# Per-image statistics moved into PSUM, gelu moved behind a unit's second bias, and the measuring steps spread out, in a fused group norm and directional convolution

## The chip, the cores and the metric

The kernel runs on one core of one Trainium2 chip. The metric is the device time of one execution, in microseconds (us). Engines are named as in the profile: PE is TensorE's matmul side, PEld its weight loads, DVE is VectorE, ACT is ScalarE, POOL is GpSimd, SP is SyncE (DMA queues have a q behind the name).

## The reference

x has the shape (16, 256, 56, 56), float32: 16 images of 256 channels.

```python
xn  = group_norm(x)                          # 32 groups of 8 channels, eps 1e-5, no affine part
h   = depthwise_conv3x3(xn, dw_weight)       # zero padding 1
h   = gelu(h)                                # the exact one
maps = einsum('bchw,oc->bohw', h, pw_weight) + pw_bias     # 256 -> 8 * 256 channels
out = x
for i, (dx, dy) in enumerate(OFFSETS8):      # the 8 neighbours
    out += maps[:, i] * (roll(xn, (dy, dx)) - xn)
```

The group norm's scale is taken out of the differences: they are made of x, and the maps are multiplied by 1/std, together with the bias.

## The kernel before

The 256 channels are two halves of 128 partitions. An image has 7 tiles of 8 rows (448 pixels); a **body** is two images, 14 tiles, and there are 8 bodies. Each engine runs its own program, written out in order by hand, and engines meet only in semaphores.

Per tile, TensorE makes eight **units** (`make_maps`, L880). A unit is a pair of directions in one half of the channels, two **sides** of 448 columns, one PSUM bank each. A side is six matmuls of 128x128 by 448: weights and h are split into a high and a low part, and three of the four products are taken for each half of the input channels. Eight units are 16 groups of six, 96 matmuls. The units use three pairs of banks in turn (`GROUPS`, L64; banks 0 to 5), with one exception: the last four units of a body take the pairs 0, 1, 0, 2. Before a unit TensorE waits until VectorE is done with the last user of its pair (L887). Banks 6 and 7 hold the convolution's sums.

ScalarE adds the bias and scales each side in place (`add_bias`, L578, the activation at L586). VectorE multiplies a unit with the difference fields, per tile in this order (L846 to L874): `first_product` of units 0 and 1, written to the sums (L690, acc); `second_product` of unit 2, written back in place (L690, psum), and `second_add`, which adds it to the sums and frees the banks (L712); `kept_product` of units 3 to 7, written to SBUF (L690, products), which GpSimd adds to the sums (`add_pair`, L365). Between these VectorE puts the eight taps of the convolution for the tile three ahead (`tap`, L770; for an image's last tile, made in its fourth, each tap is two instructions of half the size, L761).

The convolution's chain crosses the engines: ScalarE normalises x into xn (L542); the centre tap starts the sums (`start_conv`, L561; L557 in two halves); VectorE's eight taps follow; then ScalarE's gelu empties banks 6 and 7 (L571), its copy to the high part is L576, and GpSimd makes the low part (L334). gelu has to wait for the last tap, the next centre tap for gelu, and the next first tap for the centre tap. In ScalarE's body (L608 to L621) these stand behind the bias of a numbered unit:

```python
GELU_AT, START_AT, HHI_AT, NORM_AT = 0, 1, 2, 7
```

The statistics of the next image are made beside this. ScalarE measures it in twelve steps (`measure_step`, L477: sums, minus the mean, squares, variance, for each half), four in each of tiles 0, 1 and 2. VectorE then turns the moments of 128 channels into group statistics in ten small instructions on 32 or fewer columns (`group_stats`, L627 to L672: two transposes in, sums over 8, differences, their squares and sums, transposes back). They are drawn one at a time by `stats_next()`, from behind unit 6's product in tile 2 on into tile 3. All their operands are in SBUF. GpSimd makes 1/std, shift and bias of the result (`norm_scales`, L319).

GpSimd further makes the difference fields (L346, L350) and issues the DMAs that add the sums to out (L372). SyncE loads an image two ahead in the sixth tile (L286 to L289).

Of the kernel before, what the change touches and what calls it, by code (L numbers as in the profile page):

```python
# [5 lines left out]
def preact_directional_conv(nc, x, pw_t, pw_b, dw, out):  # L6
# [4 lines left out]
    P = 128  # L11
    B, C, H, W = x.shape
# [3 lines left out]
    TILES = H // ROWS  # L16
    PX = ROWS * W
# [61 lines left out]
    with ctx:  # L79
        def sb(name, shape, dt=F32):  # L80
            return ctx.enter_context(nc.sbuf_tensor(name, shape, dt))
# [46 lines left out]
        sums = sb("sums", [P, 4])  # L128
        mean_t = sb("mean_t", [P, 32])
        dev_t = sb("dev_t", [P, 32])  # L130
        devs_t = sb("devs_t", [P, 32])
        mean_b = sb("mean_b", [P, 32])
        devs_b = sb("devs_b", [P, 32])
        var_eps = sb("var_eps", [P, HALVES])
# [3 lines left out]

        psum = ctx.enter_context(nc.psum_tensor("psum", [P, 8, BANK], F32))

        def rows_of(par, g, c):
# [88 lines left out]
        MEASURES = HALVES * HALF_STEPS  # L230
        STAT = 10
        SCALES = 3
# [15 lines left out]

        GELU_AT, START_AT, HHI_AT, NORM_AT = 0, 1, 2, 7
        WRAP_AT = (4, 3)  # L250
        MEASURE_AT = ((0, 3), (0, 4), (0, 5), (0, 6), (1, 3), (1, 4), (1, 5), (1, 6), (2, 2), (2, 3), (2, 4), (2, 5))
        STATS_TILE, SCALES_TILE = 2, 3
# [192 lines left out]
        def _(act):  # L445
# [132 lines left out]
            def add_bias(n0, nl, u):  # L578

                ip, q = (nl // TILES) % 2, nl * UNITS + u  # L580
                for side in range(2):
# [5 lines left out]
                                         scale=rstd[ip][:, g:g + 1]).then_inc(biased_s, 1)  # L587

            measure_first()
            wrap(0, 0)  # L590
# [13 lines left out]
            def body(n0, b0, last):  # L604
                for nl in range(STEPS):
                    t, par = nl % TILES, nl // TILES
                    more = lambda k: not (last and nl + k >= STEPS)
                    for u in range(UNITS):  # L608
                        add_bias(n0, nl, u)
                        if (t, u) in MEASURE_AT and not (last and par):  # L610
                            measure_step(b0 + par + 1, 1 - par, MEASURE_AT.index((t, u)))
                        if u == GELU_AT and more(2):
# [13 lines left out]
        def _(dve):  # L626
            def group_stats(b):  # L627
# [4 lines left out]
                def then(ins):  # L632
                    ins.then_inc(stat, 1)
                    done[0] += 1
# [14 lines left out]
                wait()  # L649
                then(nc.vector.tensor_scalar(by8(mean_t[:]), wide(sums[:]), 1.0 / GROUP, None, ALU.mult))  # L650
                yield
                wait()
                then(nc.vector.tensor_tensor(dev_t[:], mom_t[:], mean_t[:], ALU.subtract))  # L653
                yield
                wait()
                then(nc.vector.tensor_tensor(dev_t[:], dev_t[:], dev_t[:], ALU.mult))
                yield
                wait()
                then(nc.vector.reduce_sum(sums[:], by8(dev_t[:]), axis=AX.X))
                yield  # L660
                wait()
                then(nc.vector.tensor_scalar(by8(devs_t[:]), wide(sums[:]), 1.0 / GROUP, None, ALU.mult))  # L662
                yield
                wait()
                then(nc.vector.transpose(mean_b[:], mean_t[:]))
                yield
                then(nc.vector.transpose(devs_b[:], devs_t[:]))
                yield
# [164 lines left out]
            def body(n0, b0, last):  # L833
                nonlocal stats
                for nl in range(STEPS):
# [7 lines left out]
                    if last and nl == STEPS - 1:  # L843
                        last_tile(n0, nl)
                        return
                    first_product(n0, nl, 0)  # L846
                    stats_next()
                    first_product(n0, nl, 1)
                    stats_next()
                    tap_next()  # L850
                    second_product(n0, nl)
                    tap_next()
                    second_add(n0, nl)
# [18 lines left out]
                    tap_next()  # L872
                    stats_next()
                    stats_next()  # L874

# [60 lines left out]
```

## Time and profile before

| | |
|---|---|
| three runs | 2354.85, 2356.59, 2357.29 us |
| median | 2356.59 us |
| profiled execution, its own time | 2353.0 us |
| its span in the profile | 2351.2 us |
| mean granted TensorE clock | 0.989 of full |
| PE busy | 2227.3 us, 95% |
| DVE busy | 2159.4 us, 92% |
| POOL busy | 1979.9 us, 84% |
| ACT busy | 1826.8 us, 78% |
| DMA engines | 86 GB/s on average |

The profile is of one execution; the span is what lies between its first and last instruction. Matmuls overlap, so PE's rows last longer (370 ns) than the distance from one to the next (203 ns); a group of six takes 1.22 us. A row of VectorE or ScalarE also overlaps the next by some 0.1 us.

### The profile page before, as it was taken

What the parts mean: (1) busy time and instruction counts of PE and PEld (TensorE: products, weight loads), DVE (VectorE), ACT (ScalarE), POOL (GpSimd) and SP (SyncE); (2) the same over time, 40 slices, a digit from 0 to 9 for tenths busy, and PEclk for the clock granted to TensorE, in tenths of its full rate; (3) what the DMA queues carried; (4) which work ended last, traced back from release to release, by engine and by line L of the source; (5) the groups of instructions that cost most, each with busy time, mean ns of one, the idle gap of its engine ahead of it and who ended that gap; (6) DMA issues with size and microseconds to landing.
All of it is one profiled execution on the core that took longest, in us unless ns stands there. A gap on an engine that the chain in (4) does not pass through costs nothing.

```text
span 2351.2 us, 28668 instructions
## 1 busy us (share of the span) xinstructions
PE 2227.3 (95%) x10752; PEld 2031.0 (86%) x10752; DVE 2159.4 (92%) x2218; ACT 1826.8 (78%) x2762; POOL 1979.9 (84%) x857
## 2 busy tenths in 40 slices
PE   2999999999999999999999999999999999999998
PEld 1889898898988989899898888989889898898997
DVE  7999999999999999999999999999999999999995
ACT  5968778787887968779687796877878788797775
POOL 5879898897978989799897997989879898898985
PEclk9999999999999999999999999999999999999999
DMA  6234263442725426153361643526344272543413
GB/s 187 45 71 110 48 124 73 87 95 47 159 38 102 94 48 149 32 103 93 62 135 32 118 94 66 115 45 110 89 85 96 48 151 46 95 93 51 98 32 71
DMA packets 47083, 202.13 MB, mean 86 GB/s; under 512 B 3040, under 2 KB 7136, under 8 KB 45664
## 3 DMA queue, kind: packets, MB, share of 16 engines
q0 software_dynamic: 30192, 94.97, 24.8%
q1 hardware_dynamic: 16752, 105.34, 17.3%
q8 instruction: 84, 1.38, 0.2%
q14 instruction: 55, 0.45, 0.1%
HBM read 104.88 MB, written 146.80 MB: 107 GB/s over the span
## 4 chain that ended last, share of the span: by engine, by line
PE 57%; DVE 27%; ACT 11%; issue 5%; DMA 0%; SPq 0%; DVEq 0%
PE psum L898 57%; DVE psum L770 6%; DVE products L690 6%; DVE psum L761 5%; ACT psum L586 5%; ACT squares_out L469 2%; DVE dev_t L653 2%; DVE acc L690 2%; DVE psum L690 2%; DVE acc L712 1%; ACT hid L571 1%; ACT squares_out L459 1%; DVE devs_t L662 1%; DVE var_eps L670 1%; ACT psum L561 1%
## 5 line engine op out<-in xcount | busy, mean ns | idle before, releaser
L586 ACT ACTIVATE psum<-psum,bias,rstd 128x448 f32<-128x448 f32 x1792 | 1214.0, 700 | 399.2 <-PE psum L898 396.9
L365 POOL TENSOR_TENSOR acc<-acc,products 128x896 f32<-128x896 f32 x333 | 1166.9, 3504 | 321.5 <-DVE products L690 315.0
L898 PE MATMUL psum<-hhi,w_hi 128*128 128x448 f32 x3584 | 1326.0, 370 | 117.1 <-DVE acc L690 46.1
L898 PE MATMUL psum<-hhi,w_lo 128*128 128x448 f32 x3584 | 1321.9, 369 | 0.0
L898 PE MATMUL psum<-hlo,w_hi 128*128 128x448 f32 x3584 | 1028.8, 368 | 0.3 <-POOL hlo L334 0.3
L770 DVE SCALAR_TENSOR_TENSOR psum<-xn,dw_f,psum 128x896 f32<-128x896 f32 x768 | 881.4, 1148 | 3.5
L898 PEld LDWEIGHTS psum<-hhi,w_hi 128*128 128x128 f32 x3584 | 677.9, 189 | 193.3 <-DVE acc L690 51.7
L898 PEld LDWEIGHTS psum<-hhi,w_lo 128*128 128x128 f32 x3584 | 679.7, 190 | 59.4
L898 PEld LDWEIGHTS psum<-hlo,w_hi 128*128 128x128 f32 x3584 | 677.7, 189 | 60.6 <-POOL hlo L334 0.9
L690 DVE TENSOR_TENSOR products<-psum,fields 128x896 f32<-128x896 f32 x555 | 602.1, 1085 | 49.6 <-ACT psum L586 48.2
L690 DVE TENSOR_TENSOR acc<-psum,fields 128x896 f32<-128x896 f32 x224 | 243.4, 1087 | 119.1 <-ACT psum L586 119.1
L334 POOL TENSOR_TENSOR hlo<-hid,hhi 128x896 fp32r<-128x896 f32 x112 | 264.9, 2365 | 12.9 <-ACT hhi L576 12.9
L350 POOL TENSOR_TENSOR fields<-xpad 128x896 f32<-128x896 f32 (+1 forms) x112 | 240.1, 2144 | 0.0
L346 POOL TENSOR_TENSOR fields<-xpad 128x912 f32<-128x912 f32 (+1 forms) x112 | 209.8, 1874 | 0.0
L571 ACT ACTIVATE hid<-psum 128x896 f32<-128x896 f32 x112 | 103.2, 922 | 108.8 <-DVE psum L770 71.9
L761 DVE SCALAR_TENSOR_TENSOR psum<-xn,dw_f,psum 128x448 f32<-128x448 f32 x256 | 160.4, 676 | 0.0
L372 POOL DMA_DIRECT2D out<-acc x111 | 132.8, 1197 | 7.9 <-DMA out<-acc 7.3
L690 DVE TENSOR_TENSOR psum<-psum,fields 128x896 f32<-128x896 f32 x117 | 128.4, 1098 | 5.9 <-ACT psum L586 4.7
L712 DVE TENSOR_TENSOR acc<-psum,acc 128x896 f32<-128x896 f32 x111 | 120.3, 1084 | 0.2
L542 ACT ACTIVATE xn<-xpad,shift,rstd 128x1008 f32<-128x1008 f32 (+1 forms) x96 | 116.8, 1217 | 0.0
L576 ACT CAST hhi<-hid 128x896 fp32r<-128x896 f32 x112 | 106.7, 953 | 0.0
L561 ACT ACTIVATE psum<-xn,dw_f 128x896 f32<-128x896 f32 x96 | 98.2, 1023 | 0.1
(66 smaller groups left out, 558.1 us busy)
## 6 DMA issues: line engine op xcount, KB each, us to landing
out<-acc POOLq DMA_DIRECT2D x96, 896.0 KB, 7.7
out<-x SPq DMA_DIRECT2D x16, 3136.0 KB, 12.5
xpad<-x SPq DMA_DIRECT2D x30, 1568.0 KB, 14.9
out<-acc POOLq DMA_DIRECT2D x15, 448.0 KB, 5.6
acc<-x SPq DMA_DIRECT2D x4, 784.0 KB, 7.0
xpad<-pw_t SPq DMA_DIRECT2D x1, 2048.0 KB, 12.0
out<-products SPq DMA_DIRECT2D x2, 224.0 KB, 1.9
dw_f<-dw SPq DMA_DIRECT2D x1, 9.0 KB, 8.0
```

What stands on the lines that cost most here:

```text
L334: nc.gpsimd.tensor_tensor(hlo[:, slot], hid[:], hhi[:, slot].bitcast(F32), ALU.subtract).then_inc(hlo_s, 1)
L346: nc.gpsimd.tensor_tensor(gx[:, :, f + 2 * lo:f + TR, :], v[:, :, r + 2 * lo:r + TR, 1:WP], v[:, :, r + 2 * lo:r + TR, 0:WP - 1], ALU.subt ...
L350: nc.gpsimd.tensor_tensor(gy[:, :, f + lo:f + ROWS + 1, :], v[:, :, r + lo + 1:r + TR, 1:W + 1], v[:, :, r + lo:r + ROWS + 1, 1:W + 1], AL ...
L365: nc.gpsimd.tensor_tensor(a, a, p, ALU.add).then_inc(added_s, 1)
L372: pool.dma_start(out_dst[b, :, :, t * PX:(t + width) * PX], acc[buf][:, :, sign].rearrange("p g t x -> p g (t x)"), accum_op=ALU.add).then ...
L571: nc.scalar.activation(hid[:], conv_of(n0, c), ACT.Gelu).then_inc(gelu_s, 1)
L586: nc.scalar.activation(m, m, ACT.Identity, bias=bias[ip][:, g, d:d + 1], scale=rstd[ip][:, g:g + 1]).then_inc(biased_s, 1)
L690: return nc.vector.tensor_tensor(to.rearrange("p s (r c) -> p s r c", c=W), maps(q).rearrange("p s (r c) -> p s r c", c=W), field, ALU.mult)
L712: nc.vector.tensor_tensor(a, maps(nl * UNITS + u), a, ALU.add).then_inc(prod_s, 1)
L761: nc.vector.scalar_tensor_tensor(d, xn[c % 2][:, g * TR + ky:g * TR + ky + ROWS, kx:kx + W], dw_f[:, g, TAPS_DVE[j]:TAPS_DVE[j] + 1], d, A ...
L770: nc.vector.scalar_tensor_tensor(d, xn[c % 2][:, ky:ky + 2 * ROWS, kx:kx + W].rearrange("p (a r) c -> p a r c", a=2), dw_f[:, g, TAPS_DVE[ ...
L898: last = nc.tensor.matmul(maps(q)[:, side, :], w[:, kk, col:col + P], h_part(h, t, nl, kk), start=s == 0, stop=s == len(steps) - 1)
```

## The change

It has three parts.

1. **Statistics in PSUM.** `mean_t`, `dev_t`, `devs_t` and `devs_b` leave SBUF for the 64 columns of banks 6 and 7 that the convolution leaves free (448 to 511). The squaring of the differences now takes `dev_t` from PSUM and a second copy, `dev_s`, from SBUF; making it is one more instruction (`STAT` is 11). The small instructions are drawn at other places of the tile: none stands between the last tap and the next first tap, in which time ScalarE uses banks 6 and 7.
2. **gelu** moves from behind unit 0's bias to behind unit 1's, in front of the centre tap (`GELU_AT` 0 to 1).
3. **Measuring** spreads over four tiles: three steps each in the last tile of the image before and in tiles 0, 1 and 2. For the second image the old places stay (`MEASURE_SECOND`).

```diff
-        mean_t = sb("mean_t", [P, 32])
-        dev_t = sb("dev_t", [P, 32])
-        devs_t = sb("devs_t", [P, 32])
+        dev_s = sb("dev_s", [P, 32])
         mean_b = sb("mean_b", [P, 32])
-        devs_b = sb("devs_b", [P, 32])
...
+        mean_t, dev_t, devs_t, devs_b = (psum[:, CONV_BANK + i // 2, PX + 32 * (i % 2):PX + 32 * (i % 2 + 1)]
+                                         for i in range(4))
...
-        STAT = 10
+        STAT = 11
...
-        GELU_AT, START_AT, HHI_AT, NORM_AT = 0, 1, 2, 7
+        GELU_AT, START_AT, HHI_AT, NORM_AT = 1, 1, 2, 7
...
-        MEASURE_AT = ((0, 3), (0, 4), (0, 5), (0, 6), (1, 3), (1, 4), (1, 5), (1, 6), (2, 2), (2, 3), (2, 4), (2, 5))
+        MEASURE_AT = ((-1, 4), (-1, 6), (-1, 6), (0, 3), (0, 5), (0, 5), (1, 3), (1, 5), (1, 5), (2, 3), (2, 5), (2, 5))
+
+        MEASURE_SECOND = ((0, 3), (0, 4), (0, 5), (0, 6), (1, 3), (1, 4), (1, 5), (1, 6), (2, 2), (2, 3), (2, 4), (2, 5))
...
+            def measure_at(n, u):
...
+                b, t = divmod(n, TILES)
+                if t == TILES - 1:
+                    b, t = b + 1, -1
+                if b + 1 < B:
+                    places = MEASURE_AT if b else MEASURE_SECOND
+                    for i in range(MEASURES):
+                        if places[i] == (t, u):
+                            measure_step(b + 1, (b + 1) % 2, i)
...
                         add_bias(n0, nl, u)
-                        if (t, u) in MEASURE_AT and not (last and par):
-                            measure_step(b0 + par + 1, 1 - par, MEASURE_AT.index((t, u)))
+                        measure_at(n0 + nl, u)
...
-                then(nc.vector.tensor_tensor(dev_t[:], mom_t[:], mean_t[:], ALU.subtract))
+                then(nc.vector.tensor_tensor(dev_t, mom_t[:], mean_t, ALU.subtract))
+                then(nc.vector.tensor_tensor(dev_s[:], mom_t[:], mean_t, ALU.subtract))
                 yield
                 wait()
-                then(nc.vector.tensor_tensor(dev_t[:], dev_t[:], dev_t[:], ALU.mult))
+                then(nc.vector.tensor_tensor(dev_t, dev_t, dev_s[:], ALU.mult))
...
-                then(nc.vector.transpose(mean_b[:], mean_t[:]))
-                yield
-                then(nc.vector.transpose(devs_b[:], devs_t[:]))
+                then(nc.vector.transpose(mean_b[:], mean_t))
+                then(nc.vector.transpose(devs_b, devs_t))
...
                     first_product(n0, nl, 0)
+                    first_product(n0, nl, 1)
+                    tap_next()
                     stats_next()
-                    first_product(n0, nl, 1)
+                    second_product(n0, nl)
                     stats_next()
                     tap_next()
-                    second_product(n0, nl)
-                    tap_next()
+                    stats_next()
                     second_add(n0, nl)
...
                     kept_product(n0, nl, 7)
                     tap_next()
-                    stats_next()
-                    stats_next()
```

VectorE from unit 6's product in an image's third tile to unit 2's product in the fourth, in the kernel before:

```order
L690 TENSOR_TENSOR products<-psum,fields 128x896
L770 SCALAR_TENSOR_TENSOR psum<-xn,dw_f,psum 128x2x448
L653 TENSOR_TENSOR dev_t<-mom_t,mean_t 128x32
L656 TENSOR_TENSOR dev_t<-dev_t 128x32
L690 TENSOR_TENSOR acc<-psum,fields 128x2x448
L659 TENSOR_REDUCE sums<-dev_t 128x4
L690 TENSOR_TENSOR acc<-psum,fields 128x2x448
L662 TENSOR_SCALAR devs_t<-sums 128x32
L761 SCALAR_TENSOR_TENSOR psum<-xn,dw_f,psum 128x448 x2
L690 TENSOR_TENSOR psum<-psum,fields 128x2x448
```

and the same place with the change, up to the second addition (here L705 is the product, L785 and L776 are the taps, L727 the second addition; small instructions with psum are those on mean_t, dev_t and devs_t):

```order
L705 TENSOR_TENSOR products<-psum,fields 128x896
L785 SCALAR_TENSOR_TENSOR psum<-xn,dw_f,psum 128x2x448
L705 TENSOR_TENSOR acc<-psum,fields 128x2x448 x2
L776 SCALAR_TENSOR_TENSOR psum<-xn,dw_f,psum 128x448 x2
L668 TENSOR_TENSOR psum<-mom_t,psum 128x32
L669 TENSOR_TENSOR dev_s<-mom_t,psum 128x32
L705 TENSOR_TENSOR psum<-psum,fields 128x2x448
L672 TENSOR_TENSOR psum<-psum,dev_s 128x32
L776 SCALAR_TENSOR_TENSOR psum<-xn,dw_f,psum 128x448 x2
L675 TENSOR_REDUCE sums<-psum 128x4
L727 TENSOR_TENSOR acc<-psum,acc 128x2x448
```

The first products stand together in front of the first tap, and the small instructions that stood around them come behind it. The big instructions keep their order.

ScalarE at the start of a tile, in the kernel before (L586 is the bias, two to a unit):

```order
L586 ACTIVATE psum<-psum,bias,rstd 128x448 x2
L571 ACTIVATE hid<-psum 128x896
L586 ACTIVATE psum<-psum,bias,rstd 128x448 x2
L561 ACTIVATE psum<-xn,dw_f 128x2x448
L586 ACTIVATE psum<-psum,bias,rstd 128x448 x2
L576 CAST hhi<-hid 128x896
```

and with the change (L590 bias, L575 gelu, L565 centre tap):

```order
L590 ACTIVATE psum<-psum,bias,rstd 128x448 x4
L575 ACTIVATE hid<-psum 128x896
L565 ACTIVATE psum<-xn,dw_f 128x2x448
L590 ACTIVATE psum<-psum,bias,rstd 128x448 x2
L580 CAST hhi<-hid 128x896
```

gelu has gone from between the biases of units 0 and 1 to behind both, and now stands directly in front of the centre tap that waits for it.

## Rows read from the trace of the kernel before

**Rows 1.** The list of waits: engine and line, releaser, us in total, times, longest.

```profile
PE psum L898 <- DVE acc L690: 46.1, 15, 3.4
PE psum L898 <- DVE acc L712: 24.3, 30, 2.1
```

**Rows 2.** Timeline of PE: start us, us, engine, line, operation, count [idle before, releaser].

```profile
113.68 0.57 PE L898 MATMUL psum<-hlo,w_hi 128*128 128x448 f32 x2
...
1123.98 0.47 PE L898 MATMUL psum<-hhi,w_hi 128*128 128x448 f32 x1 [3.37 <-DVE acc L690]
...
2128.64 0.57 PE L898 MATMUL psum<-hlo,w_hi 128*128 128x448 f32 x2
```

**Rows 3.** Two stretches: length, busy us per engine, granted clock, DMA share, GB/s.

```profile
1125.00:1128.40 3.40, 3.40 (x11) 3.05 (x10) 3.40 (x5) 0.88 (x2) 1.89 (x1) 0.53 0.00 0
721.62:832.02 110.40, 110.40 (x542) 101.23 (x540) 101.53 (x99) 92.27 (x139) 99.11 (x41) 1.00 0.51 104
```

**Rows 4.** Timeline of PE in an undisturbed tile: its first and sixth unit.

```profile
1035.05 0.36 PE L898 MATMUL psum<-hhi,w_hi 128*128 128x448 f32 x1
...
1047.25 0.36 PE L898 MATMUL psum<-hhi,w_hi 128*128 128x448 f32 x1
```

**Rows 5.** Timeline of DVE around the statistics of one image.

```profile
1113.18 0.20 DVE L644 STREAM_TRANSPOSE mom_t<-moments 128x32 f32<-128x32 f32 x1
1113.31 1.11 DVE L770 SCALAR_TENSOR_TENSOR psum<-xn,dw_f,psum 128x896 f32<-128x896 f32 x1
...
1115.52 0.18 DVE L650 TENSOR_SCALAR mean_t<-sums 128x32 f32<-128x32 f32 x1
...
1117.66 3.22 DVE L653 TENSOR_TENSOR dev_t<-mom_t,mean_t 128x32 f32<-128x32 f32 x1
...
1122.85 1.08 DVE L690 TENSOR_TENSOR acc<-psum,fields 128x896 f32<-128x896 f32 x1
...
1129.04 1.26 DVE L761 SCALAR_TENSOR_TENSOR psum<-xn,dw_f,psum 128x448 f32<-128x448 f32 x2
```

**Rows 6.** Timeline of POOL at the same time.

```profile
1116.78 4.05 POOL L365 TENSOR_TENSOR acc<-acc,products 128x1792 f32<-128x1792 f32 x1 [0.28 <-DVE products L690]
```

**Rows 7.** Groups by line and form: busy us, mean ns of one, idle before.

```profile
L653 DVE TENSOR_TENSOR dev_t<-mom_t,mean_t 128x32 f32<-128x32 f32 x16 | 48.5, 3033 | 0.0
L662 DVE TENSOR_SCALAR devs_t<-sums 128x32 f32<-128x32 f32 x16 | 28.4, 1775 | 0.0
L656 DVE TENSOR_TENSOR dev_t<-dev_t 128x32 f32<-128x32 f32 x16 | 27.3, 1707 | 0.5
...
L670 DVE SCALAR_TENSOR_TENSOR var_eps<-mean_b,devs_b 128x2 f32<-128x2 f32 x16 | 15.5, 971 | 0.0
...
L737 DVE TENSOR_TENSOR acc<-acc,xpad 128x896 f32<-128x896 f32 x1 | 1.1, 1082 | 0.0
```

**Rows 8.** Timeline of DVE in the undisturbed tile: units 1 and 2.

```profile
1041.21 1.09 DVE L690 TENSOR_TENSOR acc<-psum,fields 128x896 f32<-128x896 f32 x1 [1.20 <-ACT psum L586]
...
1043.38 1.10 DVE L690 TENSOR_TENSOR psum<-psum,fields 128x896 f32<-128x896 f32 x1
...
1045.44 1.08 DVE L712 TENSOR_TENSOR acc<-psum,acc 128x896 f32<-128x896 f32 x1
```

**Rows 9.** Timeline of ACT in the undisturbed tile, from the last bias of the tile before.

```profile
1035.26 0.70 ACT L586 ACTIVATE psum<-psum,bias,rstd 128x448 f32<-128x448 f32 x1 [0.52 <-PE psum L898]
...
1039.05 0.93 ACT L571 ACTIVATE hid<-psum 128x896 f32<-128x896 f32 x1 [0.66 <-DVE psum L770]
1039.87 1.31 ACT L586 ACTIVATE psum<-psum,bias,rstd 128x448 f32<-128x448 f32 x2
1041.09 1.02 ACT L561 ACTIVATE psum<-xn,dw_f 128x896 f32<-128x896 f32 x1
1042.02 1.32 ACT L586 ACTIVATE psum<-psum,bias,rstd 128x448 f32<-128x448 f32 x2
```

**Rows 10.** DMA issues of the page: KB each, us to landing.

```profile
xpad<-x SPq DMA_DIRECT2D x30, 1568.0 KB, 14.9
```

More of the change, by code:

```diff
@@ L649, in group_stats @@
                 wait()
-                then(nc.vector.tensor_scalar(by8(mean_t[:]), wide(sums[:]), 1.0 / GROUP, None, ALU.mult))
+                then(nc.vector.tensor_scalar(by8(mean_t), wide(sums[:]), 1.0 / GROUP, None, ALU.mult))
                 yield
                 wait()
-                then(nc.vector.tensor_tensor(dev_t[:], mom_t[:], mean_t[:], ALU.subtract))
+                then(nc.vector.tensor_tensor(dev_t, mom_t[:], mean_t, ALU.subtract))
+                then(nc.vector.tensor_tensor(dev_s[:], mom_t[:], mean_t, ALU.subtract))
                 yield
                 wait()
-                then(nc.vector.tensor_tensor(dev_t[:], dev_t[:], dev_t[:], ALU.mult))
+                then(nc.vector.tensor_tensor(dev_t, dev_t, dev_s[:], ALU.mult))
                 yield
                 wait()
-                then(nc.vector.reduce_sum(sums[:], by8(dev_t[:]), axis=AX.X))
+                then(nc.vector.reduce_sum(sums[:], by8(dev_t), axis=AX.X))
                 yield
                 wait()
-                then(nc.vector.tensor_scalar(by8(devs_t[:]), wide(sums[:]), 1.0 / GROUP, None, ALU.mult))
+                then(nc.vector.tensor_scalar(by8(devs_t), wide(sums[:]), 1.0 / GROUP, None, ALU.mult))
                 yield
                 wait()
-                then(nc.vector.transpose(mean_b[:], mean_t[:]))
-                yield
-                then(nc.vector.transpose(devs_b[:], devs_t[:]))
+                then(nc.vector.transpose(mean_b[:], mean_t))
+                then(nc.vector.transpose(devs_b, devs_t))
                 yield
```

## The prediction

> **What bounds the kernel now.** By the page's first part TensorE is busy for 95% of the span, so the time is TensorE's work plus its pauses. The list of waits says who pauses it inside the loop: 46.1 us in 15 waits for VectorE's first product (L690), and 24.3 us in 30 waits for the second addition at L712 [rows 1]. Fifteen is the number of images measured inside the loop, so the pauses belong to the statistics, not to the tiles.
>
> The timeline of TensorE places them: in one image a unit's first matmul comes at 1123.98 after 3.37 us idle [rows 2], and the L712 waits, 0.81 on average, follow as one in that tile and one in the next. Behind the long pause the granted clock of 1125.00 to 1128.40 is 0.53, against 1.00 in an undisturbed stretch [rows 3]: nearly all of it at the lower level, 1.2 GHz, after the engine had stood idle. From 113.68 to 2128.64, the last matmuls before the first and the fifteenth long pause [rows 2], are 14 periods, 143.93 us each. What would seven undisturbed tiles take? A tile is 16 groups of six matmuls. Ninety groups took 110.40 us from 721.62 [rows 3], 1.227 each; ten took 12.20 from 1035.05 to 1047.25 [rows 4], 1.220 each. So 112 groups take 136.6 to 137.4 us, and I take 137.1, between the two paces. **Lost are 6.8 us per image, 102 us over 15 images**: the three pauses, the refilling behind each, and the half clock.
>
> Why the long pause? VectorE's timeline beside GpSimd's gives it. L653 subtracts 32 columns in 3.22 us and ends at 1120.88 [rows 5]; GpSimd's addition, begun at 1116.78 for 4.05, ends at 1120.83 [rows 6]. L650, of the same form as the slow L662, took 0.18 at 1115.52 [rows 5], before that addition began. Over the run L653 means 3033 ns, L662 1775, L656 1707, L670 971 [rows 7]: together 7.5 us an image, for work that takes 0.2 each when unhindered. All four have only SBUF operands. Instructions with one tensor in PSUM run beside GpSimd's at their usual length all the time: the taps, L690 in place 1.10, L712 1.08 [rows 8]. Behind the four stands the product at 1122.85 [rows 5], 1.08 long, whose end lets TensorE go at 1123.98.
>
> **The change, part by part.** *Statistics.* Each instruction that was blocked now has a tensor in PSUM. I take 0.12 us of VectorE each, as L644 at 1113.18 let the tap start at 1113.31 [rows 5]. No row shows these very forms; the bounds are 0.1 and, should they block, what they cost now (1.0 to 3.2 us). I take the low end, since every form with a PSUM tensor in the trace runs at it. That is 1.3 us an image for eleven, beside VectorE's idle time of 1.20 in front of each second product [rows 8] and more behind it; if that cover went, TensorE would wait for L712 (below).
>
> A rule of the Trainium skill speaks against this: "VectorE: DVE Perf Modes", section on the TRN2 errata, gives a VectorE operation from PSUM a fixed 120 cycles where one from SBUF has 58; by it, eight small instructions per image would cost an estimated 65 ns more each, 8 us over the run if nothing hid them. The trace does not agree: an addition of 896 columns with SBUF operands alone takes 1082 ns [rows 7], the PSUM product of the same width 1.10 us [rows 8], a difference of 0.02.
>
> *Measuring.* The twelve ScalarE steps keep their durations and go to earlier tiles, at most three to one. ScalarE waits for TensorE in most units, 0.52 us before 1035.26 [rows 9], so they cost nothing; uncovered, one would delay a product by up to 1.6 us, which still has about 2 us until its banks are wanted. Where the steps begin in the seventh tile two images ahead, the load of x was issued in the sixth, behind the differences made early in it; it lands in 14.9 us [rows 10], and the step comes over 20 us after the issue. Nothing is lost.
>
> *Gelu behind the second bias.* This touches every tile, so I follow one. Its first matmul is at 1035.05, a side follows every 1.22 us, and the sixth unit, at 1047.25 [rows 4], reuses the banks that L712 frees. Now: gelu waits for the last tap until 1039.05, second bias 1039.87, centre tap 1041.09, third bias 1042.02 [rows 9], second unit's product 1041.21, third unit's 1043.38, L712 at 1045.44 for 1.08 [rows 8], ended 1046.52: 0.7 us in hand. After: the second unit is complete at 1035.05 + 4 x 1.22 = 1039.93. ScalarE starts its last bias 0.20 later, as 1035.26 stands to 1035.05: 1040.13. Gelu follows by 0.61 (the spacing of a bias and the centre tap, 1040.48 to 1041.09), 1040.74, for 0.93; the centre tap waits for it, 1041.70; the third biases come 0.93 behind, 1042.63, for 1.32, until 1043.95. Product 1043.99, L712 2.06 later as in rows 8: 1046.05, ended 1047.13. TensorE resumes 0.05 behind such an end (1123.98 against 1123.93), and the first matmul after a wait takes 0.47 for 0.36, 0.11 more [rows 2, 4]: 1047.29 against 1047.25. **So the new order loses about 0.04 us a tile, 4 us in 108 tiles**, and uses up the margin. Bounds: 0, and 0.3 if gelu's 0.93 came onto the old chain in full (0.93 less 0.7, and the restart). I take what I added up, since each link is a row.
>
> *The fourth tile of an image* has sixteen half taps. Until L712 it has one pair of halves, 1.26 against 1.11 to 1.15 for a whole [rows 5], so 0.12 more; two small instructions in front of L712, 0.24; and a centre tap in two halves on ScalarE, 0.17 more. 0.53 us, times 15 is 8 us (bounds 0 and 1.0 each). The halves and small ones behind L712, 1.2 us, fit into VectorE's idle time.
>
> *The last tile of every second image*: there the bank table puts the seventh unit onto the fifth's banks, two units back instead of three. The fifth product starts 3.06 behind L712 (one spacing of 1.00 and one of 2.06), at 1049.11 in the tile above, ends at 1050.19 and lets TensorE go by 1050.35; wanted is 1035.05 + 12 x 1.22 = 1049.69. 0.65 x 7 = 4.6 us, where the old chain just did it (bounds 0 and 1.0 each).
>
> Sum: -102 + 4 + 8 + 4.6 + 0.3 (one instruction more before the loop) = -85. The span goes from 2351.2 to 2266, the profiled execution's own time from 2353.0 to 2268; the median shown is 3.6 above that, so **2271 us**. Late next is L712 in every tile, by next to nothing, and then TensorE's own pace.
>
> **Rivals.**
> 1. *The gelu chain is some tenths longer than added up* (a link that no row shows, ScalarE held by its new neighbours). Every 0.1 a tile is 11 us; at 0.3 the time is 2304. For: no margin is left. Against: the links are measured. Chance 0.15.
> 2. *The chain is much longer, and the kernel slower.* Place: the third unit's bias, queued on ScalarE behind gelu and centre tap. From 0.8 us of lateness a tile more than added up (0.8 x 108 = 86) it takes all that the statistics give; at 1.0 the time is 2379. For: gelu and centre tap together are 1.95 us, so the price is there. Against: old and new chain hold the same instructions, and end 0.6 apart. Chance 0.04.
> 3. *Small instructions are still blocked.* If all are, the long pause and its half clock stay, 16 us of third pauses go at best and the chain's 17 come: 2357, chance 0.04. If only the multiplication by 1/8 of sums (old L662), of which no PSUM form is in the trace: it now stands ahead of a product with 1.9 us of margin, and the time is below 2285, chance 0.08.
> 4. *No pause anywhere, the chain and the tiles with halves included*: 2271 - 17 = 2254, and at the faster pace throughout 6 less, 2248. Chance 0.12.
>
> **The numbers.** The forecast itself, about 2258 to 2285, has 0.57. The range takes in rival 1 up to its 0.3, the small block of rival 3 and the upper half of rival 4: 2252 to 2302. Faster, same and slower part at 0.2%, 5 us, about what a measurement of this kernel can tell. Faster 0.92 (the forecast, rivals 1 and 4, the small block of 3), same 0.03 (most of the large block), slower 0.05 (rival 2 and the rest).
>
> **What would show it.** The statistics' lines at 0.2 us; no TensorE wait for a first product inside the loop; a granted clock of 1.00 through the fourth tile; 138 us per image; VectorE's wait of 1.20 down to about 0.5, and a new one of about 0.8 in front of the first tap; gelu without a wait for taps; the end of L712 within 0.1 us of the sixth unit's matmul; short waits for it in fourth tiles, and one for the fifth product per two images. Wrong it would be if small instructions still last over a microsecond, if TensorE waits for L712 by over 0.2 us in every tile, or if ScalarE waits for x in the seventh tile.

## The result and the profile after

| | before | after |
|---|---|---|
| runs | 2354.85 to 2357.29 us | 2269.90 to 2271.90 us (4 runs) |
| median | 2356.18 us | **2271.43 us** |
| profiled execution, its own time / its span | 2353.0 / 2351.2 us | 2271.6 / 2269.8 us |
| mean granted clock | 0.989 | 0.999 |
| PE busy | 95% | 97% |
| DVE / ACT / POOL busy | 92% / 78% / 84% | 91% / 81% / 87% |

The ratio is 0.9639 (95% interval 0.9623 to 0.9656): 3.6% faster, 0.4 us from the forecast. That the hit is so close is partly chance. The two spans differ by 81.4 us where the sum said 85, so the span came at 2269.8 where 2266 was forecast. What made up for it is the 3.6 us that the forecast added for the distance between the profiled execution of before and its median: the profiled execution of after (2271.6) lies on its median. Three executions of the kernel of experiment 5 (2344.87, 2528.48 and 2529.34 us) were disturbed as a whole and are left out of its figures.

The list of waits of after (engine and line, releaser, us in total, times, longest), which answers to [rows 1]. The old L690 is now L705, L712 is L727, L770 is L785, L586 is L590, L571 is L575.

```profile
DVE psum L785 <- ACT psum L565: 79.5, 93, 1.1
...
PEld psum L913 <- DVE acc L727: 28.3, 109, 0.7
...
ACT hid L575 <- DVE psum L785: 12.0, 2, 6.5
...
PE psum L913 <- DVE acc L727: 4.7, 15, 0.3
PE psum L913 <- DVE products L705: 2.4, 7, 0.4
```

Of 70.4 us of TensorE's waits in [rows 1] 4.7 are left, and new are seven of 0.35. No wait for a first product (L705, acc) is there. TensorE's weight load waits for L727 109 times, 0.26 on average: in every tile the second addition now ends at the last moment. gelu (L575) waits for taps twice in the whole run. The first tap of a tile (L785) waits 0.85 on average, 93 times, for the centre tap.

The timeline of TensorE answers to [rows 2, 4]. Columns as there.

```profile
118.86 0.57 PE L913 MATMUL psum<-hlo,w_hi 128*128 128x448 f32 x2
...
1055.94 0.36 PE L913 MATMUL psum<-hhi,w_hi 128*128 128x448 f32 x1
...
1068.13 0.47 PE L913 MATMUL psum<-hhi,w_hi 128*128 128x448 f32 x1
...
1087.46 0.57 PE L913 MATMUL psum<-hlo,w_hi 128*128 128x448 f32 x2
1088.32 0.47 PE L913 MATMUL psum<-hhi,w_hi 128*128 128x448 f32 x1 [0.29 <-DVE acc L727]
...
1149.51 0.57 PE L913 MATMUL psum<-hlo,w_hi 128*128 128x448 f32 x2
1150.43 0.47 PE L913 MATMUL psum<-hhi,w_hi 128*128 128x448 f32 x1 [0.35 <-DVE products L705]
...
2056.53 0.57 PE L913 MATMUL psum<-hlo,w_hi 128*128 128x448 f32 x2
```

From 118.86 to 2056.53 are again 14 images: 138.41 us each, against 143.93. Times 15 that is 82.8 us, so the loop holds the whole difference of the spans, 81.4. The short pause of 0.29 us at 1088.32 is all that is left in this tile, where before paused for 3.37. The clock does not fall behind it: the window around it (columns of [rows 3]) has a granted clock of 1.00, where before had 0.53, and so has the whole tile, 1076 to 1096.

```profile
1087.00:1092.00 5.00, 4.71 (x24) 3.99 (x23) 5.00 (x12) 2.63 (x4) 5.00 (x4) 1.00 0.01 3
```

The groups of VectorE by form answer to [rows 7]:

```profile
L672 DVE TENSOR_TENSOR psum<-psum,dev_s 128x32 f32<-128x32 f32 x16 | 3.0, 190 | 0.0
L668 DVE TENSOR_TENSOR psum<-mom_t,psum 128x32 f32<-128x32 f32 x16 | 3.0, 190 | 0.0
...
L678 DVE TENSOR_SCALAR psum<-sums 128x32 f32<-128x32 f32 x16 | 3.0, 187 | 0.0
...
L685 DVE SCALAR_TENSOR_TENSOR var_eps<-mean_b,psum 128x2 f32<-128x2 f32 x16 | 2.5, 153 | 0.0
```

The four that took 3033, 1707, 1775 and 971 ns take 190, 190, 187 and 153. VectorE's and GpSimd's timelines of one image's fourth tile show them beside GpSimd's work, which goes on without a break [rows 5, 6].

```profile
1084.20 0.19 DVE L668 TENSOR_TENSOR psum<-mom_t,psum 128x32 f32<-128x32 f32 x1
1084.30 0.18 DVE L669 TENSOR_TENSOR dev_s<-mom_t,psum 128x32 f32<-128x32 f32 x1
...
1085.81 0.19 DVE L672 TENSOR_TENSOR psum<-psum,dev_s 128x32 f32<-128x32 f32 x1
...
1087.19 1.08 DVE L727 TENSOR_TENSOR acc<-psum,acc 128x896 f32<-128x896 f32 x1
```
```profile
1083.50 2.08 POOL L350 TENSOR_TENSOR fields<-xpad 128x1140 f32<-128x1140 f32 x1
1085.55 2.00 POOL L354 TENSOR_TENSOR fields<-xpad 128x1008 f32<-128x1008 f32 x1
1087.52 2.10 POOL L338 TENSOR_TENSOR hlo<-hid,hhi 128x896 fp32r<-128x896 f32 x1
```

An ordinary tile, on ScalarE and on VectorE; these answer to [rows 8, 9], and the tile's first matmul is the one at 1055.94.

```profile
1061.02 0.70 ACT L590 ACTIVATE psum<-psum,bias,rstd 128x448 f32<-128x448 f32 x1 [0.52 <-PE psum L913]
1061.65 0.91 ACT L575 ACTIVATE hid<-psum 128x896 f32<-128x896 f32 x1
1062.65 1.01 ACT L565 ACTIVATE psum<-xn,dw_f 128x896 f32<-128x896 f32 x1
1063.60 1.30 ACT L590 ACTIVATE psum<-psum,bias,rstd 128x448 f32<-128x448 f32 x2
```
```profile
1061.75 1.09 DVE L705 TENSOR_TENSOR acc<-psum,fields 128x896 f32<-128x896 f32 x1 [0.24 <-ACT psum L590]
1063.70 1.16 DVE L785 SCALAR_TENSOR_TENSOR psum<-xn,dw_f,psum 128x896 f32<-128x896 f32 x1 [0.85 <-ACT psum L565]
1064.93 1.10 DVE L705 TENSOR_TENSOR psum<-psum,fields 128x896 f32<-128x896 f32 x1
1065.94 1.15 DVE L785 SCALAR_TENSOR_TENSOR psum<-xn,dw_f,psum 128x896 f32<-128x896 f32 x1
1066.99 1.08 DVE L727 TENSOR_TENSOR acc<-psum,acc 128x896 f32<-128x896 f32 x1
```

L727 ends at 1068.07, and the sixth unit starts at 1068.13. Counted from the tile's first matmul, the end is at 12.13, 0.07 before TensorE wants the banks (10 x 1.22 = 12.20). One line stands between the product at 1064.93 and the addition: the second tap, 1.05 us. The experiments come back to it.

### The profile page after: what moved, and what is told of

Read it like the earlier page. It is cut to its first block, busy times and chain, and to the rows that moved or that the text cites. A ratio compares the mean times of both kernels' runs of the same rounds, so it can differ in the third digit from the quotient of the medians.

```text
span 2269.8 us, 28684 instructions
## 1 busy us (share of the span) xinstructions
PE 2209.1 (97%) x10752; PEld 2008.5 (88%) x10752; DVE 2056.1 (91%) x2234; ACT 1844.6 (81%) x2762; POOL 1981.4 (87%) x857
## 4 chain that ended last, share of the span: by engine, by line
PE 88%; DVE 5%; ACT 4%; issue 2%; DMA 0%; POOL 0%; SPq 0%; ACTq 0%; DVEq 0%
PE psum L913 88%; ACT psum L590 1%; DVE psum L705 1%; ACT hid L575 1%; DVE psum L785 1%; ACT psum L561 1%; DVE acc L727 1%; DVE products L705 1%; DVE psum L776 1%; DMA acc<-x 0%; ACT psum L565 0%; DVE acc L757 0%; POOL hlo L338 0%; DVE fields L808 0%; DVE part_sums L795 0%
## 5 line engine op out<-in xcount | busy, mean ns | idle before, releaser
L590 ACT ACTIVATE psum<-psum,bias,rstd 128x448 f32<-128x448 f32 x1792 | 1205.9, 694 | 384.6 <-PE psum L913 381.9
L785 DVE SCALAR_TENSOR_TENSOR psum<-xn,dw_f,psum 128x896 f32<-128x896 f32 x768 | 883.1, 1150 | 83.0 <-ACT psum L565 79.5
L913 PEld LDWEIGHTS psum<-hhi,w_hi 128*128 128x128 f32 x3584 | 672.6, 188 | 137.1 <-issue 45.5
L913 PEld LDWEIGHTS psum<-hhi,w_lo 128*128 128x128 f32 x3584 | 672.8, 188 | 57.6
L705 DVE TENSOR_TENSOR products<-psum,fields 128x896 f32<-128x896 f32 x555 | 603.3, 1087 | 38.8 <-ACT psum L590 38.8
L705 DVE TENSOR_TENSOR acc<-psum,fields 128x896 f32<-128x896 f32 x224 | 242.6, 1090 | 53.2 <-ACT psum L590 51.8
L776 DVE SCALAR_TENSOR_TENSOR psum<-xn,dw_f,psum 128x448 f32<-128x448 f32 x256 | 161.6, 686 | 7.7 <-ACT psum L561 7.7
L705 DVE TENSOR_TENSOR psum<-psum,fields 128x896 f32<-128x896 f32 x117 | 128.6, 1100 | 17.9 <-ACT psum L590 10.8
L727 DVE TENSOR_TENSOR acc<-psum,acc 128x896 f32<-128x896 f32 x111 | 120.4, 1085 | 0.2
L575 ACT ACTIVATE hid<-psum 128x896 f32<-128x896 f32 x112 | 102.2, 913 | 12.0 <-DVE psum L785 12.0
L565 ACT ACTIVATE psum<-xn,dw_f 128x896 f32<-128x896 f32 x96 | 97.4, 1015 | 9.0 <-ACT hid L575 0.4
## 6 DMA issues: line engine op xcount, KB each, us to landing
xpad<-x SPq DMA_DIRECT2D x30, 1568.0 KB, 15.1
```

The costliest lines, as they stand in the source:

```text
L575: nc.scalar.activation(hid[:], conv_of(n0, c), ACT.Gelu).then_inc(gelu_s, 1)
L590: nc.scalar.activation(m, m, ACT.Identity, bias=bias[ip][:, g, d:d + 1], scale=rstd[ip][:, g:g + 1]).then_inc(biased_s, 1)
L705: return nc.vector.tensor_tensor(to.rearrange("p s (r c) -> p s r c", c=W), maps(q).rearrange("p s (r c) -> p s r c", c=W), field, ALU.mult)
L727: nc.vector.tensor_tensor(a, maps(nl * UNITS + u), a, ALU.add).then_inc(prod_s, 1)
L776: nc.vector.scalar_tensor_tensor(d, xn[c % 2][:, g * TR + ky:g * TR + ky + ROWS, kx:kx + W], dw_f[:, g, TAPS_DVE[j]:TAPS_DVE[j] + 1], d, A ...
L785: nc.vector.scalar_tensor_tensor(d, xn[c % 2][:, ky:ky + 2 * ROWS, kx:kx + W].rearrange("p (a r) c -> p a r c", a=2), dw_f[:, g, TAPS_DVE[ ...
```

## Experiments

Eleven kernels were run, one of them twice. The theory behind the prediction: the gain is the small instructions no longer blocked, the gelu move costs a little in every tile, and the measuring costs and gives nothing.

**1. Each part by itself.** First the measuring back at its old places, all else as after:

```diff
-                    places = MEASURE_AT if b else MEASURE_SECOND
+                    places = MEASURE_SECOND
```

> The changed kernel with the twelve measuring steps at the places of before for every image. My theory: they lie in ScalarE's waits either way: 2271.4 within 3 us. Rival, four steps in one tile delay biases and with them products: 5 us or more above.

Measured: 2271.34 us (2270.88 to 2271.97), ratio 0.9641 [0.9627, 0.9655], as after. The spreading gives nothing here, where gelu stands behind the second bias.

Then the four tiles back in SBUF, with the order of the instructions, gelu and the measuring as after:

```diff
-        mean_t, dev_t, devs_t, devs_b = (psum[:, CONV_BANK + i // 2, PX + 32 * (i % 2):PX + 32 * (i % 2 + 1)]
-                                         for i in range(4))
+        mean_t, dev_t, devs_t, devs_b = (sb(f"small{i}", [P, 32])[:] for i in range(4))
```

> The changed kernel with mean_t, dev_t, devs_t and devs_b in SBUF again, all else as changed. My theory: five or six small instructions wait for GpSimd's running one again, 1 to 3 us each; TensorE pauses for over 3 us per image and its clock falls behind that: 2350 to 2390. Rival, the new places of the small instructions in the tile brought the gain and PSUM did nothing: 2271 to 2285.

Measured: 2346.21 us (2342.71 to 2347.29), ratio 0.9954 [0.9939, 0.9969]. Its groups of VectorE by form:

```profile
L668 DVE TENSOR_TENSOR dev_s<-mom_t,small 128x32 f32<-128x32 f32 x16 | 29.3, 1831 | 0.0
L667 DVE TENSOR_TENSOR small<-mom_t,small 128x32 f32<-128x32 f32 x16 | 18.8, 1175 | 0.0
```

So the placement alone is worth 74.8 us (2346.21 - 2271.43) of the 84.8, and without it the other parts together bring 10. The new places in the tile are not what unblocked the statistics; with SBUF operands they are blocked there too, only the pause now comes at the second addition: 15 TensorE waits for it, 55.1 us in all. The time is 4 us under the range that was expected.

**2. Which forms are blocked?** Only `devs_t`, the result of the second multiplication by 1/8, goes back to SBUF. That instruction has one input tensor, not two:

```diff
+        devs_t = sb("devs_t", [P, 32])[:]
```

> The changed kernel with devs_t alone in SBUF again: L678, one input and one output in SBUF, no second tensor. My theory: it is blocked as L662 was, until the GpSimd instruction that runs at that time ends, 1 to 2 us on average, and as a product with 1.9 us of margin stands behind it, the time is 2271 to 2285. Rival, only instructions with two SBUF tensors as inputs are blocked: L678 at 0.19 us and 2271.4 within 2.

Measured: 2276.09 us (2275.29 to 2277.23), ratio 0.9661 [0.9647, 0.9676]. VectorE's group and its timeline, and GpSimd's:

```profile
L679 DVE TENSOR_SCALAR devs_t<-sums 128x32 f32<-128x32 f32 x16 | 18.3, 1141 | 0.0
```
```profile
1089.88 1.54 DVE L679 TENSOR_SCALAR devs_t<-sums 128x32 f32<-128x32 f32 x1
```
```profile
1089.28 2.10 POOL L339 TENSOR_TENSOR hlo<-hid,hhi 128x896 fp32r<-128x896 f32 x1
```

It ends at 1091.42, GpSimd's subtraction at 1091.38: the whole of the wait is that subtraction, and in all 15 images L679 ends 0.04 behind it. This form is blocked as well, and one such instruction costs 4.7 us over the run (2276.09 - 2271.43). In the kernel before, the sum over 8 (L647) and the transpose in front of it (L644, 0.20 us at 1113.18 [rows 5]) have only SBUF operands too, and run in the middle of a GpSimd addition without waiting for it:

```profile
1111.29 4.08 POOL L365 TENSOR_TENSOR acc<-acc,products 128x1792 f32<-128x1792 f32 x1 [1.52 <-DVE products L690]
```
```profile
1114.33 0.17 DVE L647 TENSOR_REDUCE sums<-mom_t 128x4 f32<-128x32 f32 x1
```

The Trainium skill has this in "SBUF — State Buffer", section "Who interferes with whom": an exclusive lock on a port pair shared with GpSimd, taken by a tensor_tensor with both inputs in SBUF (beside a GpSimd instruction that reads SBUF) and by a tensor_scalar in a two-port mode, never by tensor_reduce. By that rule the four tiles went to the right place, and these runs agree, 1141 ns for 32 columns among them. No transpose of these small tiles took over 0.22 us in any of the traces.

**3. What does the gelu move do, in the old kernel?** Before, with gelu behind the second bias and nothing else:

```diff
-        GELU_AT, START_AT, HHI_AT, NORM_AT = 0, 1, 2, 7
+        GELU_AT, START_AT, HHI_AT, NORM_AT = 1, 1, 2, 7
```

> The kernel before with gelu alone moved behind unit 1's bias. My theory: long pause, half clock and the pause at 0.8 us stay; the pause of the fifth tile (1.1 x 15 = 16 us) goes, 0.04 x 108 and 0.6 x 7 come: about 2348, between 2340 and 2360. Rival, the gelu move carries a good part of the 85 us: under 2320.

Measured: 2356.07 us (2354.77 to 2358.66, ten runs), ratio 1.0 [0.9991, 1.0009]. The expected gain of some 8 us did not come. Its waits, and the window behind the long pause of one image:

```profile
PE psum L898 <- DVE acc L690: 51.7, 15, 3.7
...
PE psum L898 <- DVE acc L712: 7.0, 10, 2.2
```
```profile
1128.00:1131.40 3.40, 3.40 (x11) 2.99 (x10) 3.40 (x5) 0.70 (x1) 2.01 (x1) 0.50 0.00 0
```

The waits for L712 fall from 24.3 us to 7.0: the pauses in the tile behind are gone, as expected. The long one grew, 46.1 to 51.7 in total, and the mean granted clock is lower, 0.985 for 0.989. Counted on TensorE from one tile's first matmul to the next's, on average over 14 images, the fifth tile of an image takes 19.67 us where before took 20.70, but the fourth 25.88 for 25.31, the last 19.95 for 19.59, and the other four about 0.07 more each: 1.0 us saved and 1.2 paid. The step that the expectation lacked is the longer fourth tile. A wait that goes can be paid back by the one beside it.

**4. The price of the gelu move without statistics.** Two kernels leave the statistics out from the second image on (VectorE only signals that they are done): before, and after.

```diff
+            def no_stats(b):
+
+                dve.wait_ge(measure, b * MEASURES + MEASURES)
+                dve.sem_inc(stat, STAT)
+                yield
...
-                        stats = iter(group_stats(b0 + par + 1))
+                        stats = iter(no_stats(b0 + par + 1))
```

> The kernel before without the ten small instructions for all images but the first (their semaphore is raised in one step; the later images are normalised with the first one's statistics); measuring stays. My theory: long pause, half clock and the pause in fourth tiles come from the small instructions and go, of the fifth tile's pause half stays: 2356 - 102 + 8 = 2262, between 2256 and 2268, with a granted clock of 1.00. Rival, the half clock comes once per image without the pause: 20 us more, about 2282. Second rival, the half taps cause the two pauses at L712 by themselves: 2275 or more.

> The changed kernel without the small instructions for all images but the first (as e5_before_no_stats). My theory: of the pause in fourth tiles (0.56 each) the 0.24 of the two small instructions in front of L727 goes, the rest is the gelu chain's: 2271.4 - 15 x 0.24 = 2267.8, between 2265 and 2270; against 2255.6 with gelu first this is the gelu move's own price, 12 us. Rival, the gelu chain costs nothing and the statistics are all that is left: 2256 to 2260.

Measured: before without statistics 2255.59 us (2255.20 to 2255.90), ratio 0.9574 [0.9558, 0.959]; after without them 2268.95 (2267.99 to 2269.45), 0.9633 [0.9619, 0.9647]. The first is just under the range expected. The statistics of before therefore cost 101 us (2356.18 - 2255.59), where the prediction had 102. Those of after cost 2.5. And the two kernels without statistics differ by **13.4 us**. They differ in the order of gelu and in the places of measuring, and measuring cost nothing in experiment 1, so the order of gelu is the likely price; the run that would part the two for certain (no statistics, gelu behind the second bias, measuring at the old places) was not made. Tile by tile (as in 3) the price lies in the fourth tile, 19.97 for 19.63 us, in the last, 19.95 for 19.61, and 0.04 in each of the others. The forecast had priced just this: 4 + 8 + 4.6 us, less 3.6 for the two small instructions, is 13.

**5. So put gelu back, with the small tiles in PSUM?** After, with one number changed:

```diff
-        GELU_AT, START_AT, HHI_AT, NORM_AT = 1, 1, 2, 7
+        GELU_AT, START_AT, HHI_AT, NORM_AT = 0, 1, 2, 7
```

> The changed kernel with gelu back behind unit 0's bias; statistics in PSUM and the new places of measuring stay. My theory: the gelu move did not bring the gain, it only lengthened every tile's chain by 0.6 us. Undone, L727 ends about 0.5 us before the sixth unit wants its banks, the 0.04 us per tile, the pause of the last tile of every second image (7 of 0.6) and most of the pause in fourth tiles (15 of 0.56) go, together 15 us; but in the fifth tile of an image gelu then waits for the late half taps, and up to 0.6 x 15 = 9 us come back there. 2263 to 2268. Rival, the move was needed: the third pause of 1.1 us per image returns in full and nothing goes, 2280 or more.

Measured: 2270.66 to 2272.31 us, ratio 0.964 [0.9624, 0.9656], where a gain was expected. It was run again, to read where the time lies:

> The same kernel as e1_gelu_first, which took 2272.15 us where I expected 2263 to 2268 and whose profile shows a disturbed TensorE. Time: 2272 again. What its profile is to tell: where the 16 us over e5_before_no_stats (2255.59, also gelu first) lie. Account A: in the fifth tile of an image gelu waits for the last half tap, the second bias stands behind gelu, and TensorE pauses for L727 by about 1 us, once per image. Account B: in the fourth tile, by the small instructions in front of L727. Account C: a little in every tile.

Measured: 2270.45 and 2271.76 us, ratio 0.9643 [0.9623, 0.9662]; span 2270.0 us against 2269.8. The moved gelu brings nothing in this kernel either, nor does it cost. The trace says why: two pauses stand in place of the small ones. The waits, and TensorE in the fourth tile and in the fifth:

```profile
ACT hid L575 <- DVE psum L785: 89.0, 82, 6.5
...
PE psum L913 <- DVE acc L727: 8.3, 21, 0.6
```
```profile
1088.69 0.47 PE L913 MATMUL psum<-hhi,w_hi 128*128 128x448 f32 x1 [0.49 <-DVE acc L727]
...
1108.02 0.57 PE L913 MATMUL psum<-hlo,w_hi 128*128 128x448 f32 x2
1108.64 0.47 PE L913 MATMUL psum<-hhi,w_hi 128*128 128x448 f32 x1
```

gelu behind the first bias waits for the last tap in most tiles (82 times, 1.1 us on average), and all biases queue behind it. In an undisturbed tile there is room for that. Where small instructions or halves make the last tap late, the lateness reaches the biases and TensorE. Against before without statistics the fourth tile is 0.74 us longer and the fifth 0.34, the others hardly: accounts B and A, together 16 us over 15 images. Behind the second bias gelu waits for a tap only twice in the whole run of after; but its own 0.91 us stands in front of the third bias always. The two orders cost the same here, in different tiles.

The new places of measuring make taps late as well: the last tap of an image's third tile ends 4.57 us into the tile in after and 4.23 in the first run of experiment 1, which differs from it in these places alone. In after it costs nothing; gelu behind the first bias waits for that tap. No run has gelu first, the small tiles in PSUM and the old places of measuring, so how much of the fourth tile's pause is measuring's stays open.

**6. Other orders of after.** The convolution one unit later (`START_AT` 2, VectorE's first tap behind unit 3's product), so that the second addition has nothing between it and its product:

```diff
-        GELU_AT, START_AT, HHI_AT, NORM_AT = 1, 1, 2, 7
+        GELU_AT, START_AT, HHI_AT, NORM_AT = 1, 2, 2, 7
...
-                    tap_next()
-                    stats_next()
                     second_product(n0, nl)
-                    stats_next()
-                    tap_next()
-                    stats_next()
                     second_add(n0, nl)
...
```

> The changed kernel with the centre tap behind unit 2's bias (START_AT 2) and VectorE's first tap behind unit 3's product, so that the second product and the second addition wait neither for gelu nor for the centre tap. My theory: L727 ends about 1.6 us before the sixth unit wants its banks, all short pauses inside the loop go: 2271.4 - 17 = 2254, between 2250 and 2259. Rival, VectorE now idles 2.3 us per tile in front of the second product where it has 2.0 to give, and taps become late: 2270 to 2290.

Measured: 2289.64 us (2289.15 to 2290.03), ratio 0.9716 [0.97, 0.9732], the rival's side. A line of its waits, and TensorE in the fourth tile:

```profile
PE psum L913 <- DVE acc L705: 16.9, 31, 0.7
```
```profile
1093.11 0.47 PE L913 MATMUL psum<-hhi,w_hi 128*128 128x448 f32 x1 [0.47 <-DVE acc L705]
```

All eight taps now stand behind unit 3's product or later. In what is left of the tile they come too late, gelu waits for them even behind the second bias (62 waits for L785, 57.2 us), and the *first* products are late: the late engine is the same, the place moved.

Next the small instructions were taken out of the part of the tile where L727 is due. They now begin behind the second addition of tile 2, and all are over before the fourth tile's first product (`MEASURE_AT` is moved forward so that the moments are there in time). The first lines of the edit:

```diff
                     tap_next()
-                    stats_next()
                     second_product(n0, nl)
-                    stats_next()
                     tap_next()
-                    stats_next()
                     second_add(n0, nl)
+                    if t == STATS_TILE and not (last and par) and b0 + par > 0:
+                        stats = iter(group_stats(b0 + par + 1))
                     stats_next()
...
```

> The changed kernel with measuring finished in an image's second tile and all small instructions of the statistics drawn behind L727 of the third tile. My theory: the fourth tile has no small instruction in front of L727 any more, all else stays: 2266 to 2269. Rival, small instructions are as dear in the third tile: 2271 or more.

Measured: 2268.26 us (2267.75 to 2268.84), ratio 0.9631 [0.9616, 0.9645], 3 us under after, and TensorE's 15 waits for L727 are gone from the list, which leaves out the shortest ones: the fourth tile still takes 19.97 us, for 20.16 in after and 19.66 in an ordinary tile. It ends where after without any statistics ends (2268.95, fourth tile 19.97): hidden so, and with gelu behind the second bias, the statistics are free.

On top of it, gelu behind the first bias in all tiles but the fifth:

```diff
-                        if u == GELU_AT and more(2):
+                        if u == (1 if t == 4 else 0) and more(2):
```

> As e9_stats_in_third_tile, with gelu behind unit 0's bias in all tiles but an image's fifth, where it stays behind unit 1's. My theory: no gelu chain at its margin (12 us), no small instruction in front of L727, no gelu that holds up a bias for late half taps: 2255 to 2260, as fast as the kernel without statistics. Rival, account C or B holds: 2264 to 2272.

Measured: 2264.66 us (2263.78 to 2264.92), ratio 0.9614 [0.9598, 0.963], a miss by 5 us. One pause per image stayed, in the fourth tile, 0.46 us at its sixth unit. ScalarE early in that tile:

```profile
1077.28 0.92 ACT L575 ACTIVATE hid<-psum 128x896 f32<-128x896 f32 x1 [1.28 <-DVE psum L785]
```

Gelu starts 4.99 us into the tile (first matmul at 1072.29), where before without statistics has 4.35 on average. The small instructions of the third tile make its last tap late, into the fourth, and gelu passes that on, as in 5.

**7. The line between product and addition.** This leaves gelu behind the second bias and the statistics in the third tile, and moves one tap, from in front of the second addition to behind unit 4's product, where VectorE has time. The small instructions are also drawn from one product later on:

```diff
                     second_product(n0, nl)
-                    tap_next()
                     second_add(n0, nl)
...
                     kept_product(n0, nl, 4)
                     stats_next()
                     tap_next()
                     stats_next()
+                    tap_next()
+                    stats_next()
                     kept_product(n0, nl, 5)
```

> As e9_stats_in_third_tile (gelu behind unit 1's bias in all tiles), with VectorE's second tap drawn behind the second addition instead of in front of it. My theory: L727 comes 1.0 us earlier in every tile and 1.2 earlier in the fourth, the fifth product of the last tile 0.9 earlier, so no short pause is left inside the loop: 2268.3 - 11 = 2257 if TensorE's pace stays between its two values, 2255 to 2256 if it goes at 1.227 us per group throughout as in e5_before_no_stats (2255.59), which paused nowhere; between 2250 and 2260. Rival, the product behind the addition waits for its bias and the second addition for the second product, so the lateness only moves: 2264 or more.

Measured: **2253.76 us** (2251.22 to 2254.74, five runs), ratio 0.9563 [0.955, 0.9576]: 17.7 us under after, and as fast as before without statistics, with the statistics in it. The list of waits has no L727 any more. VectorE, ScalarE and TensorE in the fourth tile of an image, whose first matmul is at 1069.30 (the bias behind the fourth group starts at 1074.40, 5.10 later, for 5.08 in after):

```profile
1078.50 1.10 DVE L705 TENSOR_TENSOR psum<-psum,fields 128x896 f32<-128x896 f32 x1 [0.51 <-ACT psum L590]
1079.70 1.09 DVE L727 TENSOR_TENSOR acc<-psum,acc 128x896 f32<-128x896 f32 x1
```
```profile
1074.40 0.70 ACT L590 ACTIVATE psum<-psum,bias,rstd 128x448 f32<-128x448 f32 x1 [0.53 <-PE psum L917]
```
```profile
1081.57 0.36 PE L917 MATMUL psum<-hhi,w_hi 128*128 128x448 f32 x1
```

The addition follows its product by 1.20 instead of 2.06 and ends at 1080.79, 0.78 before TensorE wants the banks, in the very tile that was late in all the other kernels with statistics. The saving against the third-tile version is 14.5 us where 11 was expected. This version beats both kernels.

## Why the prediction was right

**The bound and the 102 us.** Right. Before without statistics is 101 us faster, and its TensorE has no wait in the loop. Seven tiles of after take 112 x 1.2238 = 137.1 us where 137.1 was taken; 1.2238 is the mean over the trace.

**The statistics' lines.** Right in kind: none is blocked, the tensor_scalar neither, so both blocks of rival 3 are out. They take 0.15 to 0.21 us by their rows, and the next instruction starts 0.10 behind (L668 to L669), so the 0.12 of the sum holds. The same subtraction with SBUF operands alone, unblocked, is in the trace of before without statistics, for the first image:

```profile
L653 DVE TENSOR_TENSOR dev_t<-mom_t,mean_t 128x32 f32<-128x32 f32 x1 | 0.2, 192 | 0.0
```

With operands in PSUM it takes 190 (L668). The rule of the Trainium skill that the prediction weighs, on the page "VectorE: DVE Perf Modes", section on the TRN2 errata, would make that an estimated 65 ns more; no trace here shows it.

**The half clock.** Right: 1.00 through the fourth tile.

**Gelu behind the second bias.** The mechanism and each link were right. Counted from the tile's first matmul, the second unit's last bias was put at 5.08 and came at 5.08, gelu 5.69 and 5.71, centre tap 6.65 and 6.71, third bias 7.58 and 7.66, L712's end 12.08 and 12.13. What was mis-sized is the last term: 0.04 a tile, 4 us, measured about 0.08, some 8 us. The links were 0.05 later together, and a matmul let go on time still takes the long 0.47 once its weight load has waited. Per image 138.41 - 137.07 = 1.34 are lost; the fourth tile takes 0.56 of it (1087.46 to 1088.32 is 0.86 where 0.41 is usual, and 0.11 for the restart), the last tile of every second image 0.62, half of that per image; the remaining 0.47 are in some six tiles.

**The fourth tile, the last tile.** 0.53 was said for the fourth, or 0.57 with the 0.04 of every tile, and 0.56 measured. One part of it can be checked: without the two small instructions, for which 0.24 was taken, the tile is 0.19 shorter (20.16 to 19.97). 0.65 was said for the last tile of every second image, and 0.62 measured, seven times, for the fifth product as named.

**Measuring.** Right: nothing either way.

**The waits.** The first product's wait of 1.20 was to fall to 0.5 and is 0.24, half of that; the new one in front of the first tap was to be 0.8 and is 0.85. The load of x still lands after 15.1 us (14.9 in [rows 10]), and ScalarE waits for no x.

**Rivals 1, 2 and 4.** The chain was 0.04 longer than added up, not 0.3 or 0.8. Rival 4, no pause at all, was given 2254 at mixed pace; the change did not reach it, but the version of experiment 7 did, at 2253.76. The prediction took the second tap as given between product and addition, because the change left it there; it had not asked whether it needs to be. The prediction priced the gelu move at 16.6 us, 13 of them without the small instructions, where 13.4 were measured. What it did not ask is whether the move is worth that price. The pauses in fifth tiles that it takes away, some 16 us, are part of the 102 us; experiment 3 shows that in the old kernel the move gains nothing on balance, experiment 5 that in the new one nothing is lost without it. The move pays for itself and no more.

## What to carry to other kernels

A tiny VectorE instruction costs what the GpSimd instruction beside it still has to run, if it is of a form that is blocked (here both inputs in SBUF, or a tensor_scalar between SBUF tensors): look in the groups by form for a small shape with a large mean, and give it one operand in PSUM. When a chain then ends exactly when it is due, list what stands in it that need not: here one tap between a product and its addition, worth 14.5 us where hiding the statistics better was worth 3. And test the parts of a change one by one, since of three parts here one carried the gain (74.8 of 84.8 us), one did nothing, and one cost as much as it saved. The other 10 us belong to none of them alone; what is left for them is the new places of the small instructions, which no run tested by themselves.

## What was not expected of the hardware

TensorE without a wait runs at one of two paces. Two stretches of experiment 7, each of 222 groups of six matmuls (columns of [rows 3]):

```profile
599.28:871.60 272.32, 272.32 (x1334) 249.81 (x1332) 253.03 (x274) 227.44 (x342) 244.08 (x107) 1.00 0.46 92
1424.20:1695.04 270.84, 270.84 (x1333) 249.75 (x1332) 252.97 (x274) 227.40 (x342) 244.55 (x107) 1.00 0.46 92
```

That is 1.2267 us a group in one and 1.2200 in the other, 204.4 and 203.3 ns a matmul, at the same granted clock of 1.00 and the same load on every engine. The pace stays for the whole stretch, and in this trace it changes only at a short wait. In after, where nearly every tile has one, the mean of 1.2238 says that both occur about equally. Before without statistics goes at 1.227 in nine tenths of its groups, 1.2260 on average, and loses some 11 us by it (1792 groups x 0.0060). So kernels that differ by a few us may differ in pace as well: the same kernel with gelu second, at 1.2237, is 13.4 us slower although it gains 4 by its pace. Which restart gives which pace, and why, stays open: no run here forced the one or the other.
